# A recurrent block with layer norm and a ternary feed-forward on one core: low parts earlier, casts and products on other engines, a split output projection

## The reference, cut to what matters

```python
xn = layernorm(x)
# branch 1: gated linear recurrence
y    = gelu(xn @ w_y + b_y)
xb   = xn @ w_x + b_x
conv = conv_b + sum(conv_w[k] * shifted(xb, 3 - k) for k in range(4))
gate_x, gate_a = sigmoid(conv @ w_ig + b_ig), sigmoid(conv @ w_ag + b_ag)
log_a = -8 * gate_a * softplus(a_param)
a, mult = exp(log_a), sqrt(1 - exp(2 * log_a))      # first token: a = 0, mult = 1
h[t]  = a[t] * h[t-1] + (gate_x * conv * mult)[t]
attn  = (h * y) @ w_out + b_out
# branch 2: feed-forward of 682 hidden units, ternary weights q(w)
ffn   = (silu(xn @ q(w1).T) * (xn @ q(w3).T)) @ q(w2).T
out   = x + attn + ffn
```

## Time and profile before

| | us |
|---|---|
| median of 3 runs | 75.48 |
| lowest, highest | 75.25, 76.12 |
| the profiled execution, its own time | 75.99 |
| its span, from the first to the last instruction | 74.2 |
| busy: TensorE, VectorE, ScalarE, GpSimd | 69.2, 61.2, 48.3, 31.5 |

### The profile page before, as it was taken

The page is one execution under the profiler, slowest core; times in us unless marked ns, Lnnn a source line. Parts: engine busy times, 40 slices in busy tenths (PEclk is TensorE's granted clock), DMA queues, the critical chain, the costliest instruction groups (busy, mean ns, idle before and its releaser), DMA issues.

```text
span 74.2 us, 1064 instructions
## 1 busy us (share of the span) xinstructions
PE 69.2 (93%) x364; PEld 58.6 (79%) x364; DVE 61.2 (82%) x101; ACT 48.3 (65%) x75; POOL 31.5 (43%) x43
## 2 busy tenths in 40 slices
PE   4999969999999999999999999999999999999920
PEld 4985758877888888888888888888899999988800
DVE  4897499999999999999979974697960799999750
ACT  3674523899999999999998978466699910000000
POOL 6385647245851680016002979947689000000000
PEclk9999999999999999999999999999999999999999
DMA  0889999920000000000000000000000000000195
GB/s 8 236 289 333 368 379 342 379 97 9 0 0 0 4 0 0 0 0 0 4 1 0 0 9 0 0 0 0 0 0 0 0 0 0 9 0 0 61 322 183
DMA packets 5095, 5.63 MB, mean 76 GB/s; under 512 B 525, under 2 KB 4578, under 8 KB 5090
## 3 DMA queue, kind: packets, MB, share of 16 engines
q1 hardware_dynamic: 4946, 5.55, 22.1%
q10 hardware_dynamic: 144, 0.01, 0.1%
HBM read 4.51 MB, written 1.05 MB: 75 GB/s over the span
## 4 chain that ended last, share of the span: by engine, by line
PE 80%; DMA 7%; DVE 5%; SPq 3%; issue 1%; DVEq 0%
PE slot L664 25%; PE slot L647 23%; PE slot L696 14%; PE slot L706 8%; DMA x_sb<-x 7%; PE slot L767 4%; PE slot L673 2%; SPq L186 2%; DVE stats L436 2%; PE slot L740 2%; DVE x_sb L551 1%; PE slot L636 1%; DVE xt_lo L455 1%; SPq L183 1%; DVEq L52 0%
## 5 line engine op out<-in xcount | busy, mean ns | idle before, releaser
L256 POOL TENSOR_TENSOR g_lo<-w_raw,g_hi 128x512 fp32r<-128x512 f32 x10 | 14.1, 1421 | 9.0 <-ACT g_hi L338 8.9
L664 PE MATMUL slot<-xt_hi,w_q 128*128 128x512 f32 x40 | 15.7, 393 | 0.0
L664 PE MATMUL slot<-xt_lo,w_q 128*128 128x512 f32 x40 | 15.7, 393 | 0.0
L514 DVE SCALAR_TENSOR_TENSOR w_raw<-w_raw,s,slot 128x512 f32<-128x512 f32 x10 | 7.3, 747 | 3.1 <-ACT w_raw L332 3.0
L696 PE MATMUL slot<-w_q,g_hi 128*128 128x256 f32 x40 | 9.7, 283 | 0.0
L696 PE MATMUL slot<-w_q,g_lo 128*128 128x256 f32 x40 | 9.7, 283 | 0.0
L492 DVE SCALAR_TENSOR_TENSOR conv<-slot,par,conv 128x511 f32<-128x511 f32 (+2 forms) x12 | 9.0, 748 | 0.4
L664 PEld LDWEIGHTS slot<-xt_hi,w_q 128*128 128x128 f32 x40 | 7.5, 188 | 1.7
L664 PEld LDWEIGHTS slot<-xt_lo,w_q 128*128 128x128 f32 x40 | 7.5, 188 | 1.7
L332 ACT ACTIVATE w_raw<-slot,scale 128x512 f32<-128x512 f32 x10 | 6.6, 684 | 3.1 <-PE slot L664 3.1
L696 PEld LDWEIGHTS slot<-w_q,g_lo 128*128 128x128 f32 x40 | 7.7, 192 | 0.0
(11 more groups left out here) (111 smaller groups left out, 144.5 us busy)
## 6 DMA issues: line engine op xcount, KB each, us to landing
w_raw<-w13t SPq DMA_DIRECT2D x2, 682.0 KB, 7.6
w_raw<-dense SPq DMA_DIRECT2D x5, 256.0 KB, 5.6
out<-x_sb SPq DMA_DIRECT2D x3, 256.0 KB, 2.2
w_raw<-w2t SPq DMA_DIRECT2D x1, 640.0 KB
x_sb<-x SPq DMA_DIRECT2D x4, 128.0 KB, 2.3
x_sb<-x SPq DMA_DIRECT2D x1, 512.0 KB, 5.3
out<-x_sb SPq DMA_DIRECT2D x2, 128.0 KB, 2.1
w_raw<-w2t SPq DMA_DIRECT2D x2, 42.0 KB
```

The costliest lines, as they stand in the source:

```text
L256: nc.gpsimd.tensor_tensor(g_lo[:, j, s], g[:, n % RING], g_hi[:, j, s].bitcast(f32), ALU.subtract).then_inc(g_lo_set, 1)
L514: nc.vector.scalar_tensor_tensor(out=g[:, n % RING], in0=silu[:, n % RING], scalar=s32[:, 0:1], in1=slot[H_SLOT[s][j]][:, 1], op0=ALU.mult ...
L664: mm = nc.tensor.matmul(slot[H_SLOT[s][j]][:, o], w13_q[:, c, col:col + P], v[:, s, c], start=(c == 0 and v is xt_hi), stop=(c == KC - 1 a ...
```

## The change

1. VectorE: `xt_lo_of(0)` stands ahead of the second sequence's statistics. The second norm goes in two halves, with the load of x split in two. The epsilon addition goes to GpSimd. The first three columns of the convolution are written by VectorE (`first_columns`) and not corrected afterwards; the bias sums on GpSimd (`tap_sum`) are cut around `rstd_of`.
2. The paddings of `gt` and the rate constants go from VectorE to GpSimd. The high parts of w_ig and w_ag go from ScalarE to GpSimd, and w_out gets a high and a low part there. The low part of w_y is made in two halves, after the second norm.
3. ScalarE runs one Gelu on a single column early, takes over the tail's two casts, and leaves the last `g_hi` to GpSimd. The cast of b_out comes later.
4. TensorE: the first product takes the low parts of the first half between the high parts; the y product takes w_lo last; two small warm-up products go and one of 64 columns comes.
5. Tail: roots and states of the first sequence, and states and decays of the second, lie in three free PSUM banks (`state`). The second sequence's `gated_products` run on GpSimd. `hy` gets a high part (ScalarE) and a low part (GpSimd), and `project` is made of three float32r products, for the second sequence bank by bank. The fourth store is issued by ScalarE.

```diff
+        hy_hi, hy_lo = conv_hi, conv_lo
...
+        S_BANK = (slot[1][:, 1], slot[2][:, 0], slot[2][:, 1])
+
+        def state(s, c):
+
+            return S_BANK[(KC * s + c) % len(S_BANK)]
...
-            sp.dma_start(x_sb[:, 1], x_dram[1]).then_inc(x_loaded[TILES], 16)
+            for i in range(2):
+                t = slice(i * TILES // 2, (i + 1) * TILES // 2)
+                sp.dma_start(x_sb[:, 1, t], x_dram[1][:, t]).then_inc(x_loaded[TILES + i], 16)
...
-            for n, (s, i) in enumerate(O_ALL):
-                sp.wait_ge(o_set, n + 1)
-                t = slice(O_TILES[s][i].start, O_TILES[s][i].stop)
-                sp.dma_start(out_dram[s][:, t], x_sb[:, s, t]).then_inc(out_stored, 16)
+            for n in (0, 1, 2, 4):
+                store(sp, n)
...
             def rstd_of(s, tiles, ready):
+                pool.wait_ge(mv_set, TILES * s + tiles.stop)
+                nc.gpsimd.tensor_scalar(v_eps[:, s, tiles], mv[:, s, tiles, 1], EPS, None, ALU.add).then_inc(v_set, 1)
...
+            tap_biases()
+            tap_sum(0)
             rstd_of(0, slice(0, TILES // 2), 1)
             rstd_of(0, slice(TILES // 2, TILES), 2)
+            for i in range(1, TAPS):
+                tap_sum(i)
             pool.wait_ge(xn_set, TILES)
             square_lo(WX)
-            rstd_of(1, slice(0, TILES), 3)
-            square_lo(WY)
-            square_lo(WIG)
-            square_lo(WAG)
+            rstd_of(1, slice(0, TILES // 2), 3)
+            rstd_of(1, slice(TILES // 2, TILES), 4)
+            pool.wait_ge(xn_set, 2 * TILES)
+            for c in range(KC):
+                square_lo(WY, range(c, c + 1))
+            for m in (WIG, WAG):
+                square_hi(m)
+                square_lo(m)
+            lo_of_conv(0, 0)
+            half_biases()
+            rates()
+            lo_of_conv(0, 1)
+            gt_pads(slice(32, HALF), 1.0, KC)
+            pool.wait_ge(gt_pads_set, 1)
+            lo_of_conv(1, 0)
+            gt_pads(slice(96, P), 0.0, KC + 1)
+            pool.wait_ge(gt_pads_set, 2)
+            lo_of_conv(1, 1)
+            pool.wait_ge(a2_set, SEQS)
+            square_hi(WOUT)
+            square_lo(WOUT)
+            for n in range(2 * FULL):
+                if n == 2 * FULL - 1:
+                    pool.wait_ge(g_set, n + 1)
+                    nc.gpsimd.tensor_copy(g_hi[:, HJ[n][1], HJ[n][0]], g[:, n % RING]).then_inc(g_hi_set, 1)
+                lo_of_g(n)
...
+                nc.gpsimd.tensor_tensor(tx[:, 1, c], tx[:, 1, c], mult[:, 1, c], ALU.mult).then_inc(nx1_set, 1)
+
+            for c in range(KC):
+                gated_products(c)
             for s in range(SEQS):
                 for c in range(KC):
...
+                    pool.wait_ge(hy_hi_set, KC * s + c + 1)
+                    nc.gpsimd.tensor_tensor(hy_lo[:, s, c], tx[:, s, c], hy_hi[:, s, c].bitcast(f32), ALU.subtract).then_inc(hy_lo_set, 1)
...
             square_hi(WX)
             xt_hi_of(0)
+            act.wait_ge(quarter_set, 2)
+            nc.scalar.activation(gelu_in[:, 1:2], gelu_in[:, 0:1], ACT.Gelu)
             square_hi(WY)
             newest_tap(0)
-            square_hi(WIG)
             xt_hi_of(1)
...
+            g_hi_of(2 * FULL - 2)
+            silu_of(2 * FULL - 1)
             for s in range(SEQS):
                 for c in range(KC):
                     mult_of(s, c)
+            act.wait_ge(g_set, 2 * FULL)
+            nc.scalar.activation(state(1, 0), ta[:, 1, 0], ACT.Copy).then_inc(a_psum, 1)
+            hy_hi_of(0, 0)
+            nc.scalar.activation(state(1, 1), ta[:, 1, 1], ACT.Copy).then_inc(a_psum, 1)
+            hy_hi_of(0, 1)
+            hy_hi_of(1, 0)
+            hy_hi_of(1, 1)
+            store(act, 3)
...
-            nc.vector.memset(gt[32:HALF].bitcast(f32), 1.0).then_inc(gt_pads_set, 1)
-            nc.vector.memset(gt[96:P].bitcast(f32), 0.0).then_inc(gt_pads_set, 1)
...
+            def gated_products(c):
+
+                dve.wait_ge(nx_step, 1)
+                dve.wait_ge(mult_set, c + 1)
+                nc.vector.tensor_tensor(state(0, c), tx[:, 0, c], state(0, c), ALU.mult).then_inc(nx_set, 1)
 
             def scan(s, c):
 
...
+                nc.vector.tensor_tensor_scan(state(s, c), a, nx, 0.0, ALU.mult, ALU.add).then_inc(h_set, 1)
...
-            dve.wait_ge(x_loaded[TILES], 16)
-            statistics(1, range(TILES))
-            variance(1, range(TILES))
             xt_lo_of(0)
-            normalise(1, range(TILES), 3)
...
+            for i in range(2):
+                dve.wait_ge(x_loaded[TILES + i], 16)
+                statistics(1, tile_halves[i])
+                variance(1, tile_halves[i])
+            normalise(1, tile_halves[0], 3)
+            first_columns(0, 0)
+            normalise(1, tile_halves[1], 4)
             older_taps(0, 0)
             xt_lo_of(1)
...
+                    for k, (v, w, ready) in enumerate(((hy_hi, w_hi, hy_hi_set), (hy_hi, w_lo, hy_hi_set), (hy_lo, w_hi, hy_lo_set))):
+                        pe.wait_ge(ready, KC * s + c + 1)
+                        for i in banks:
+                            for t in O_TILES[s][i]:
+                                mm = nc.tensor.matmul(out_tile(s, i, t), v[:, s, c, t * P:(t + 1) * P], w[:, WOUT, c],
+                                                      start=False, stop=(c == KC - 1 and k == 2), skip_group_check=True)
...
             pe.wait_ge(w_hi_set, WX + 1)
-            first_x_terms((w_hi,), xt_hi, xt_hi_set)
-            pe.wait_ge(w_lo_set, WX + 1)
-            first_x_terms((w_lo,), xt_hi, xt_hi_set)
-            first_x_terms((w_hi,), xt_lo, xt_lo_set).then_inc(xb_psum, 1)
+            first_x_terms((w_hi,), xt_hi, xt_hi_set, 0)
+            first_x_terms((w_hi,), xt_lo, xt_lo_set, 0)
+            first_x_terms((w_hi,), xt_hi, xt_hi_set, 1)
+            pe.wait_ge(w_lo_set, KC * (WX + 1))
+            for h in range(2):
+                first_x_terms((w_lo,), xt_hi, xt_hi_set, h)
+            first_x_terms((w_hi,), xt_lo, xt_lo_set, 1).then_inc(xb_psum, 1)
             pe.wait_ge(w_hi_set, WY + 1)
...
+            dense_terms(slot[Y_SLOT[0]], WY, [(w_hi, xt_hi[:, 0]), (w_hi, xt_lo[:, 0])], True, False)
+            transposes(1, first_half)
+            transposes(1, second_half)
+            pe.wait_ge(w_lo_set, KC * WY + 1)
+            dense_terms(slot[Y_SLOT[0]], WY, [(w_lo, xt_hi[:, 0])], False, True, chunks=[0])
+            pe.wait_ge(w_lo_set, KC * WY + 2)
+            dense_terms(slot[Y_SLOT[0]], WY, [(w_lo, xt_hi[:, 0])], False, True, chunks=[1]).then_inc(y_psum, 1)
...
-            for s in range(SEQS):
-                project(s)
+            pe.wait_ge(w_lo_set, KC * (WOUT + 1))
+            project(0, range(len(O_TILES[0])))
+            for i in range(len(O_TILES[1])):
+                project(1, [i])
```

235 lines of the change are left out of this document (126 added, 109 removed).

## The result

The changed kernel takes 74.67 us (median of 11 runs, 74.29 to 74.95), against 75.58 us for the kernel before in the same sessions (75.25 to 76.17, 11 runs): a ratio of 0.987, 95% interval 0.984 to 0.990. It is faster, by 0.9 us and not by the 2.5 us forecast; 74.67 lies above the range of 72.4 to 74.2 us. The profiled execution took 74.64 us around a span of 72.8 us (before: 75.99 and 74.2 us). Before's profiled execution lay some 0.4 us above its median, so the traces differ by 1.4 us where the medians differ by 0.9 us.

What follows compares the result with a forecast made beforehand. TensorE's unbroken stream and its two unfilled ends were taken to bound the kernel. Head 1.1, middle -0.1 and tail 1.45 us sum to 2.45, rounded to 2.5, giving a median of 73.0 us, range 72.4 to 74.2.

Steps and rivals of the forecast that it cites:

- Head, 1.1 us: Start of the kernel: low parts of x ahead of the second norm gain 0.75 to 1.37 us, taken as 1.1.
- my two cases for the second half: Head: second half's normalisation starts at 6.35 us if GpSimd's epsilon addition is let in at once, 6.85 if it waits.
- Projection, 1.15 us: Tail: 48 split products in 5.76 us replace 32 fp32 records in 6.93 us, a gain of 1.15 us.
- Stores, 0.3 us: Behind TensorE's end: one store on ScalarE's queue removes about 0.3 us before the last store; the 2.0 us landing stays.
- Middle: 0 to 0.9 us lost; I take 0.1 us: TensorE's full stretch: work moved to GpSimd and ScalarE costs 0 to 0.9 us, taken as 0.1.
- TensorE's deadlines there come 1.84 us apart, and none is reached: Middle, hidden products: casts moved between ScalarE and VectorE make TensorE wait nowhere, with eight records per 1.84 us.
- Rival A: Middle: GpSimd and VectorE exclusion delays convolution low parts or ternary weights, 0.5 to 0.9 us more wait, 73.7 us; chance 0.15.
- A slack of 0.1 to 0.3 us, thin, and I let it stand at zero cost: Tail: the last low part of hy is ready at 66.5 us, TensorE asks for it at 66.6; no wait counted.
- Rival B: Tail hand-over: a GpSimd instruction late by its length, 1.29 us, makes TensorE wait about 1.1 us, 74.1 us; chance 0.12.
- D: Tail: scans with PSUM operands at half rate add 4.9 us to VectorE's chain, 77.7 us; chance 0.04.
- C: Head gains nothing, through ScalarE's Gelu load or late GpSimd powers; only the tail is left, 74.0 us; chance 0.09.
- a side condition: Tail: each VectorE instruction has one operand in PSUM, so by the skill's rule it does not contend with GpSimd.

Runs made afterwards that it cites:

- the first experiment: Changed kernel with the last silu ahead of the ninth cast of g on ScalarE: 74.35 us, ratio 0.985 to the kernel before.
- the kernel with the early cast: Changed kernel with ScalarE's first tail cast moved ahead of the cast of g 2: 73.99 us, ratio 0.982 to the kernel before.
- the two last kernels: Changed kernel with four edits (last silu, tail subtraction, head order, last low part on VectorE): 73.32 us; the same with the output weight's split later: 73.35 us.

## Why the prediction was wrong

- **Direction and bound: right.** The kernel is bound by TensorE's stream and what lies behind it, and the change is faster.
- **Head, 1.1 us: 0.95 us between the two traces.** No wait for the low parts of x was left, ScalarE's Gelu load (8.45 us, its next activation at 9.74) was in time, and the second sequence's first product came at 15.04 us, the late end of 14.45 to 15.05. Of my two cases for the second half, neither was right: GpSimd's epsilon addition got in between the two normalisations, and the second half's normalisation started at 6.57 us, between my 6.35 and 6.85. Taking the order back (75.78 us) shows that the mechanism is this order.
- **Projection, 1.15 us: 1.10 us,** at 0.12 us a record. Two slips nearly cancel here: 6.93 - 5.76 is 1.17 and not 1.15, and 6.93 us was a window that ended at 70.85 us, before the last record; the whole projection took 7.07 us, and the split one would take 5.97 without its wait. **Stores, 0.3 us: 0.6 us**, half of it a shorter landing that I had not expected.
- **"Middle: 0 to 0.9 us lost; I take 0.1 us": the first step that failed; 0.68 us.** I had the exclusion of rows 7 in hand and set it against GpSimd's new work ahead of 32 us, where it cost TensorE nothing. I did not carry it to the output weight's split at 38 us, which falls on the gated input. I counted the tail's casts as work that VectorE loses and ScalarE gains, without asking what stands in front of what afterwards: ScalarE's first cast stands ahead of silu 4, and the 2.16 us subtraction moved ahead of g 5. "TensorE's deadlines there come 1.84 us apart, and none is reached" was an assertion; the deadline of g 5 was not worked out. Rival A had size and kind right (0.5 to 0.9 us of exclusion in the middle) and the place wrong.
- **"A slack of 0.1 to 0.3 us, thin, and I let it stand at zero cost": the second; 0.62 us.** The chain was set at its earliest (load at 53.1 us, from a TensorE 1.4 us ahead), and the projection at its earliest too, but the chain slipped 0.65 us more than the projection did. I had overlooked that ScalarE's order has the cast of g 8 ahead of the last silu; 0.3 us of the wait are that (the first experiment). The rest of the 0.65 us is not taken apart. Rival B had the place right and half the price; its cause, a GpSimd instruction late by its own length, is not what happened.
- **Sum.** 2.45 us forecast; 0.58 more than reckoned was lost in the middle, 0.62 in the projection's wait, 0.15 in the head and 0.05 in the projection's work, and the stores gave 0.29 back: 1.34 us, the difference of the traces (1.36 us).
- **From the traces to the medians: 0.5 us, a third error.** I read all terms from an execution 0.5 us above its median and took the same 0.5 us off again for the changed kernel. Its profiled execution lay at its median (74.64 and 74.67 us), so the traces' 1.4 us are only 0.9 us between medians. Where the kernel before lost its 0.4 us is not shown, since it has one trace. The likely place is the head: other profiled executions 0.5 to 0.6 us above their median have the late head (32.69 us in the kernel with the early cast, and 32.36 against 31.81 us in the two last kernels, which have the same head). If so, the head is worth about 0.5 us between medians, half of the 1.1 us forecast (my estimate: 0.91 us of the medians, plus the 0.18 us lost behind the head, minus 0.59 us behind TensorE's end).
- **D** (slower by the scan in PSUM) is excluded: scans took 1.22 to 1.23 us there. **C** too, as far as the Gelu load and the powers go. What I had as a side condition, that the chain be free of the exclusion through one operand in PSUM, turned out to be the part that everything rests on: without it, 81.27 us. The Trainium skill ("SBUF — State Buffer", "Who interferes with whom") has this rule, and the two traces agree: 0.69 us with one SBUF input, 1.53 us with two. The section excepts the 2-port modes from this rule and counts `tensor_scalar` among the instructions that can enter one. I left that out in the prediction, though the held normalisation of rows 7 is a tensor_scalar; no run here shows the mode itself.

What stays open: the tail's casts were not put back on VectorE by themselves, so their own worth is not measured; where the kernel before lost the 0.4 us of its profiled execution; and the difference of 0.3 us between the change and the kernel with the fp32 projection is about what two medians of some runs can differ by.

## What to carry to other kernels

A gain in one stage must be followed to the end through each engine's queue: here 1.3 us of 2.6 us were lost again in two places, both visible as one gap between TensorE's starts. Moving one instruction in a queue removed the first and swapping two halved the second; giving the last subtraction to VectorE took most of the rest. Compare profiled executions from a common landmark (here the start of the hidden products), since one head alone starts them up to 0.9 us apart. Where GpSimd and VectorE share the work, ask of each pair that may overlap whether the VectorE instruction reads two SBUF tensors; if it does, add the overlap to the one that comes second, and put one operand in PSUM or change the order. A slack thinner than the estimate's own error is a term of the sum and not a zero.
